# Low and high parts for two more small products, a later place for them, and another order of the low parts, in a four-layer kernel on one core

## Chip, cores and metric

The kernel runs on one core of a Trainium2 chip, in one launch. The metric is the device time of that core in microseconds (us), median over runs. TensorE is written PE in the profile, VectorE DVE, ScalarE ACT, GpSimd POOL and SyncE SP.

## What is computed

The input `x` has 4 sequences of 1024 tokens with 512 features, all float32. Four layers with residual sums follow each other. Cut to what matters here:

```python
x = x + L0(x)     # 512 -> 2048 -> 512, gelu, a part of fc2 chosen per sequence
x = x + L1(x)     # 512 -> 512, weight chosen per sequence
x = x + L2(x)     # below
x = x + L3(x)     # 512 -> 512, weight chosen per sequence

# L2
wg = sigmoid([x, ema(x)] @ Wg.T + bg);  gated = x * wg
h1 = gelu(x @ Wn1.T + bn1)                            # 128 wide
mod = 0.5 + sigmoid(h1 @ Wn2.T + bn2)                 # 4 rates
traces[d] = ema_d(gated * mod[d])                     # 4 scans along the tokens
temporal = sum_d softmax(blend)[d] * traces[d]
gate = sigmoid(temporal @ Wtemp.T + btemp)
soma = gelu(x @ Wsoma.T + bsoma)
out = (soma * gate) @ Wout.T
return (out - mean(out)) / sqrt(var(out) + 1e-5) * gamma + beta
```

## The kernel before

Features lie on the 128 partitions, in 4 chunks, and tokens in the free dimension, in 8 tiles of 512 tokens (tiles 0 to 7, `LAST` is 7). A float32 product is made of three products of a faster kind: each operand is split into a high part (`hi`, rounded by ACT) and a low part (`lo`, the rest, by a subtraction on DVE), and `split_product` adds hi*hi, hi*lo and lo*hi in one bank of PSUM (lines 1623 to 1625). Every engine's program is written out by hand in the order in which it runs, and waits on semaphores for the others.

L0 and L1 of all tiles come first, up to about 690 us. Then L2 and L3 run in rounds. Round r (the loop `for r in range(2, NT)` stands in the programs of ACT and DVE, `range(1, NT)` in that of PE) holds, on PE: `n1(r)` (x @ Wn1), `gate(r, 0)` with the small product `mo(r)` (h1 @ Wn2) in it, the temporal layer `te` of tile r-1, `gate(r, 1)`, `gate(r, 2)`, L3 of tile r-2, `gate(r, 3)`, `ou` of tile r-1, `so(r)` and, between its banks, `ss(r-1)`, a product with ones that sums the squares of `out` over the features. A `gate(i, m)` takes 12 products for one half of the tokens, 12 for the context and 12 for the other half, each 256 wide.

On DVE a round has the four scans of each of 4 chunks (`traces_a` to `traces_d`: `gated_of`, and for each rate `drive_of`, `trace_of`, `add_of`), and between them the low parts, `spikes` (soma * gate, which frees a bank of `te`), `sum_squares`, and `z_of` and `x3_of` for the output of the layer. For the first tile of a sequence `trace_of` starts from zero, for the second from the last column of the first (`trace_last`).

What is not split before: `mo` of tiles 0, 1 and 2 (line 1780, plain float32, as soon as `h1` is there) and `ss` of tile 0 (line 1958). For tiles 3 to 7 `mo` is split: ACT makes `h1_hi` (L1181), DVE `h1_lo` (`h1_low`, L2119). It stands behind the 12 context products of `gate(i, 0)`, not ahead of them. `temporal_low(r, 0)` and `temporal_low(r, 2)` make the low parts of chunks 0, 1 and of chunks 2, 3 of `temporal`; `te_part` waits for the pair that holds its chunk. `te(i, m)` goes through all four chunks for one bank m. The high parts are `temporal_hi(r, m)`. In the profile digits are left out of names: `h` is `h1`, `h_hi` is `h1_hi`, `h_lo` is `h1_lo`, `wn_hl` stands for `wn1_hl` and `wn2_hl`.

The modulation goes to the other engines through DRAM: ACT makes `mod_row` (`mod_of`, `modulation_out`), stores it, and loads it into `mod_t` for all partitions (`modulation_back`, L1200). `drive_of` waits for that load. Two waits of PE at the change: `gate(r, 1)` waits for `spikes(r-1, 0)`, and `l1(LAST, 0)`, L1 of the last tile, which follows `gate(1, 0)`, waits for the four `x1_lo(LAST, c)`.

Of the kernel before, what the change touches and what calls it, by code (L numbers as in the profile page):

```python
# [5 lines left out]
F32 = mybir.dt.float32  # L6
# [37 lines left out]
def build(nc, x, tok16, tok8, small, fc1_w, fc2_w, exp_w, exp_b, l1_w, l1_b, wg, wn1, wsoma, wtemp, wout,  # L44
# [16 lines left out]
    with ctx:  # L61
# [419 lines left out]
        def ss_bank(i):  # L481
            return bank[5 if i == LAST - 1 else 0]
# [27 lines left out]
        def mo_split_no(i):  # L510
            return max(0, i - 2)

        def ss_split_no(i):
            return i
# [440 lines left out]
        def _(eng):  # L955
# [58 lines left out]
            modulation_back(0)  # L1014
            last_columns(0, 0)
# [4 lines left out]
            on.wait_ge(s_made, len(MADE))  # L1020
            eng.memset(wn2_hl[:, :, :].bitcast(F32), 0.0).then_inc(s_wn2, 1)
# [4 lines left out]
        def _(eng):  # L1026
# [151 lines left out]
            def h1_hi_of(i):  # L1178
                on.wait_ge(s_h1, i + 1)
                on.wait_ge(s_pe["SS"], i - 1)  # L1180
                eng.activation(h1_hi[:, :], h1[:, :], ACT.Copy).then_inc(s_h1hi, 1)  # L1181
# [76 lines left out]
            def o_of(i, m):  # L1258
                ps = te_bank(m)
                on.wait_ge(s_pe["OU"], KC * i + m + 1)  # L1260
                if 0 < i < LAST - 1:
                    on.wait_ge(s_pe["L3"], KC * i)
                elif i == LAST - 1:
                    on.wait_ge(s_pe["WG"], KC * NT)
                elif i == 0:
                    for c in range(KC):
                        on.wait_ge(s_hl7[c], 16)
                if i == LAST:
                    if m == 0:
                        on.wait_ge(s_pe["SS"], LAST)  # L1270
                    on.wait_ge(s_add, SH * KC * NT)
                    eng.activation(square_of(i, m), ps[:, :], ACT.Square).then_inc(s_sq, 1)
                    eng.activation(o_of_tile(i)[:, m, :], ps[:, :], ACT.Copy).then_inc(s_o, 1)
                    return
                eng.activation(o_of_tile(i)[:, m, :], ps[:, :], ACT.Copy).then_inc(s_o, 1)
                on.wait_ge(s_o, KC * i + m + 1)
                if m == 0:
                    if i:
                        on.wait_ge(s_pe["SS"], i)
                        on.wait_ge(s_pe["MO"], min(i + 2, NT))  # L1280
                    eng.activation(sumsq[:, :], ps[:, :], ACT.Square).then_inc(s_sq, 1)
                else:
                    if i == LAST - 1:
                        on.wait_ge(s_pe["WG"], KC * NT)
                    eng.activation(square_of(i, m), ps[:, :], ACT.Square).then_inc(s_sq, 1)
# [206 lines left out]
            for c in range(KC):  # L1492
                x1_hi(LAST, c)
            h1_of(1)
            mod_of(1)
# [23 lines left out]
            on.wait_ge(s_wn2, 1)  # L1519
            eng.activation(wn2_hl[:, 0, 0:TAUS], wn2_sb, ACT.Copy).then_inc(s_wn2, 1)  # L1520
            soma_of(1, 0)
            soma_of(1, 1)
# [6 lines left out]
            for r in range(2, NT):  # L1529
                if r == 2:  # L1530
                    h1_of(r)
                    temporal_hi(r - 1, 3)
                else:
                    temporal_hi(r - 1, 3)
                    h1_of(r)
                    h1_hi_of(r)
# [81 lines left out]
        def _(eng):  # L1618
# [151 lines left out]
            def mo(i):  # L1770
                if i > 2:

# [13 lines left out]
            def gate(i, m):  # L1786
# [43 lines left out]
                if m == 0 and i:  # L1830
                    gate_tokens(i, m, 0, 1)
                    if i < 3:
                        mo(i)
# [5 lines left out]
                if m == 0 and i > 2:  # L1839
                    mo(i)  # L1840
# [29 lines left out]
            def te_two(i, m, chunks=range(KC)):  # L1870
                for b in (m, m + 1):
                    if b >= HALF:
                        on.wait_ge(s_soma, KC * i + b + 1)
# [70 lines left out]
            def ss(i):  # L1944
# [6 lines left out]
                if i:  # L1951
                    on.wait_ge(s_ssqhi, ss_split_no(i))
                    eng.matmul(ss_bank(i)[:, :], ones[:, :], sumsq_hi_of(i), start=True, stop=False)  # L1953
                    on.wait_ge(s_ssqlo, ss_split_no(i))
                    eng.matmul(ss_bank(i)[:, :], ones[:, :], sumsq_lo[:, :], start=False, stop=True  # L1955
                               ).then_inc(s_pe["SS"], 1)
                    return
                eng.matmul(ss_bank(i)[:, :], ones[:, :].bitcast(F32), sumsq[:, :], start=True, stop=True
# [112 lines left out]
            for r in range(1, NT):  # L2071
                if r > 1:
                    n1(r)
                    gate(r, 0)
                    for m in range(KC):
                        te(r - 1, m)
# [38 lines left out]
        def _(eng):  # L2115
# [565 lines left out]
            traces_d(0, 3)  # L2681
# [9 lines left out]
            first_traces(1, 0)  # L2691
            x2_of(LAST, 3)
            first_sum(1, 0)
# [19 lines left out]
            traces_c(1, 2)  # L2713
# [3 lines left out]
            traces_c(1, 3)  # L2717
            traces_d(1, 3)
            on.wait_ge(s_wn2, 2)
            low_part(wn2_hl[:, 1, 0:TAUS], wn2_sb, wn2_hl[:, 0, 0:TAUS]).then_inc(s_wn2, 1)  # L2720
            temporal_low(1, 0)
            temporal_low(1, 2)
            for r in range(2, NT):
                if r > 2:
                    h1_low(r)
# [42 lines left out]
                if r == LAST:  # L2768
                    temporal_low(r, 0)
                traces_d(r, 3)  # L2770
                if r < LAST:
                    temporal_low(r, 0)
# [96 lines left out]
```

## Time and profile before

| | |
|---|---|
| median of 3 runs | 1280.25 us (1280.19 to 1282.09) |
| profiled execution | 1279.87 us, span of its trace 1278.1 us |
| PE busy | 1268.8 us, 99% of the span |
| DVE busy | 1067.0 us, 83% |
| ACT busy | 721.6 us, 56% |
| POOL busy | 79.6 us, 6% |
| granted PE clock | 0.999 of full speed |

The page's second part shows that DVE is fuller in the second half, with 9 tenths and more in most slices from 23 on. A product's own row shows it from its start to a modelled end and overlaps the next; how long the engine spends on it is read from start to start.

### The profile page before, as it was taken

The numbers are of one execution on the slowest core, as the hardware profiler recorded it, in microseconds if no ns is written. First come the engines' busy times: TensorE is split into PE (matmuls) and PEld (weight loads), VectorE is DVE, ScalarE is ACT, GpSimd is POOL, SyncE is SP. The second block draws the span as 40 slices with busy tenths as digits, with TensorE's granted clock in tenths as the row PEclk, the third lists the DMA queues.
The fourth block names the chain that finished last, engine by engine and source line by source line (L and its number), as shares of the span: only waits on it lengthen the run. The fifth ranks groups of instructions, "written<-read, shape, count | busy, mean of one in ns | idle before, by whom it ended". The sixth has DMA issues, their size and how long they took to land. (4 is left out here: it accounts for less than half of the span.)

```text
span 1278.1 us, 17514 instructions
## 1 busy us (share of the span) xinstructions
PE 1268.8 (99%) x6109; PEld 1066.8 (83%) x6109; DVE 1067.0 (83%) x1685; ACT 721.6 (56%) x1371; POOL 79.6 (6%) x118
## 2 busy tenths in 40 slices
PE   9999999999999999999999999999999999999998
PEld 7788888888888888888888888888888888888887
DVE  7977777787786987786875898999999999998984
ACT  7577565776475875475765253453636353636355
POOL 0010000000000000000001211002100210021000
PEclk9999999999999999999999999999999999999999
DMA  8357653648744657644749887956467555754401
GB/s 294 103 167 236 191 182 132 222 158 255 225 163 150 239 181 255 201 169 148 239 137 354 306 332 264 391 209 238 174 212 265 196 217 196 260 202 167 140 17 67
DMA packets 115151, 263.68 MB, mean 206 GB/s; under 512 B 10440, under 2 KB 32968, under 8 KB 109944
## 3 DMA queue, kind: packets, MB, share of 16 engines
q1 hardware_dynamic: 95200, 184.32, 42.1%
q10 hardware_dynamic: 15032, 62.45, 13.9%
q0 software_dynamic: 4832, 15.79, 3.3%
q8 instruction: 49, 0.80, 0.3%
q14 instruction: 38, 0.31, 0.1%
HBM read 182.24 MB, written 80.28 MB: 205 GB/s over the span
## 5 line engine op out<-in xcount | busy, mean ns | idle before, releaser
L1623 PE MATMUL bank<-h_hl,w_hl 128*128 128x512 f32 x512 | 199.4, 389 | 0.0
L1624 PE MATMUL bank<-h_hl,w_hl 128*128 128x512 f32 x512 | 199.2, 389 | 0.0
L1625 PE MATMUL bank<-h_hl,w_hl 128*128 128x512 f32 x512 | 199.2, 389 | 0.0
L1623 PE MATMUL bank<-t_hi,sp_hl 128*128 128x512 f32 x448 | 175.2, 391 | 3.2 <-DVE u_sb L2176 1.0
L1624 PE MATMUL bank<-t_lo,sp_hl 128*128 128x512 f32 x448 | 174.4, 389 | 0.0
L1625 PE MATMUL bank<-t_hi,sp_hl 128*128 128x512 f32 x448 | 174.4, 389 | 0.0
L1623 PEld LDWEIGHTS bank<-h_hl,w_hl 128*128 128x128 f32 x512 | 96.1, 188 | 21.0 <-issue 1.2
L1625 PEld LDWEIGHTS bank<-h_hl,w_hl 128*128 128x128 f32 x512 | 96.1, 188 | 20.1
L1624 PEld LDWEIGHTS bank<-h_hl,w_hl 128*128 128x128 f32 x512 | 96.1, 188 | 19.8
L1623 PEld LDWEIGHTS bank<-t_hi,sp_hl 128*128 128x128 f32 x448 | 84.1, 188 | 24.0 <-issue 2.2
L1625 PEld LDWEIGHTS bank<-t_hi,sp_hl 128*128 128x128 f32 x448 | 84.1, 188 | 17.6
L1624 PEld LDWEIGHTS bank<-t_lo,sp_hl 128*128 128x128 f32 x448 | 84.1, 188 | 17.1
L2356 DVE SCALAR_TENSOR_TENSOR drive<-gated,small_sb,mod_t 128x512 f32<-128x512 f32 x128 | 92.5, 744 | 3.3 <-DVE gated L2343 0.7
L2119 DVE TENSOR_TENSOR w_hl<-w_raw,w_hl 128x512 fp32r<-128x512 f32 x128 | 86.7, 685 | 4.3 <-ACT w_hl L1067 3.9
L1134 ACT ACTIVATE h_hl<-hb_in 128x512 fp32r<-128x512 f32 x64 | 40.2, 628 | 82.3 <-DMA hb_in<-hb_dram 55.4
L1067 ACT ACTIVATE w_hl<-w_raw 128x512 fp32r<-128x512 f32 x128 | 78.3, 619 | 6.3 <-PE bank L1625 6.3
L2367 DVE TENSOR_TENSOR_SCAN drive<-alpha,trace_last,drive 128x512 f32<-128x512 f32 x64 | 80.2, 1275 | 0.5
L2367 DVE TENSOR_TENSOR_SCAN drive<-alpha,drive 128x512 f32<-128x512 f32 x64 | 76.4, 1214 | 0.4
L1000 POOL COPY trace_last<-drive 128x1 f32<-128x1 f32 x64 | 48.1, 752 | 412.5 <-DVE drive L2367 411.1
L1051 ACT ACTIVATE sp_hl<-s_raw_sb 128x256 fp32r<-128x256 f32 x128 | 50.9, 411 | 38.4 <-PE bank L1625 36.9
L1624 PE MATMUL bank<-x_slot,wg_hl 128*128 128x256 f32 x256 | 72.4, 283 | 0.0
L1625 PE MATMUL bank<-x_slot,wg_hl 128*128 128x256 f32 x256 | 72.4, 283 | 0.0
(236 smaller groups left out, 3053.9 us busy)
## 6 DMA issues: line engine op xcount, KB each, us to landing
wg_hl<-wg_dram ACTq DMA_DIRECT2D x24, 1536.0 KB, 8.3
fc_raw<-in_fc_w SPq DMA_DIRECT2D x32, 512.0 KB, 4.1
hb_dram<-hb_out SPq DMA_DIRECT2D x64, 256.0 KB, 2.3
hb_in<-hb_dram ACTq DMA_DIRECT2D x64, 256.0 KB, 4.2
x2hl_dram<-x_hl POOLq DMA_DIRECT2D x28, 512.0 KB, 5.4
x_slot<-x2hl_dram SPq DMA_DIRECT2D x26, 512.0 KB, 4.4
wg_hl<-wg_dram SPq DMA_DIRECT2D x8, 1536.0 KB, 8.9
stage<-in_l_w SPq DMA_DIRECT2D x32, 256.0 KB, 3.4
```

What stands on the lines that cost most here:

```text
L1000: eng.tensor_copy(trace_last[:, TAUS * c + d:TAUS * c + d + 1], traced[:, TOK - 1:TOK]).then_inc(s_tracel, 1)
L1051: eng.activation(sp_hl[n % RING][:, 0, :, :], product_source(n), ACT.Copy).then_inc(s_shi, 1)
L1067: eng.activation(w2_hl[v % 3][:, 0, :, :], w2_raw[:, j, :, :], ACT.Copy).then_inc(s_w2hi, 1)
L1134: eng.activation(h_hl[v % 4][:, 0, :], hb_in[v % 4][:, :], ACT.Copy).then_inc(s_hhi, 1)
L1623: eng.matmul(ps, w_hi, x_hi, start=first, stop=False, skip_group_check=resumed)
L1624: eng.matmul(ps, w_hi, x_lo, start=False, stop=False, skip_group_check=resumed)
L1625: return eng.matmul(ps, w_lo, x_hi, start=False, stop=final, skip_group_check=resumed)
L2119: return eng.tensor_tensor(lo, raw, hi.bitcast(F32), ALU.subtract)
L2356: eng.scalar_tensor_tensor(drive[d % 2][:, :], gated[:, :], blend_sb[:, TAUS * c + d:TAUS * c + d + 1], mod_t[:, d, :], ALU.mult, ALU.mult ...
L2367: eng.tensor_tensor_scan(traced, alpha[:, 1 + d:2 + d].to_broadcast([P, TOK]), traced, start, ALU.mult, ALU.add).then_inc(s_trace, 1)
```

## The change

1. `mo` of tiles 1 and 2 is split and stands behind the context products, as that of the later tiles. That needs `h1_hi(1)` and `h1_hi(2)` on ACT, `h1_low(1)` and `h1_low(2)` on DVE, and the split of Wn2 (`wn2_hl`) before `mo(1)`: the memset on POOL, the copy on ACT and the subtraction on DVE move ahead.
2. `ss(0)` is split: `sumsq_hi(0)` on ACT between `soma_of(1, 0)` and `soma_of(1, 1)`, `sumsq_low(0)` on DVE behind `trace_of(1, 2, 2)`.
3. `te` of tile 1 (round 2) goes by two banks at a time, chunk by chunk (`te_two`), as the last tile's does.
4. On DVE `temporal_low(r, 0)` moves ahead of `traces_d(r, 3)`, and `h1_low(r + 1)` from the start of the next round to between `traces_d(r, 3)` and `temporal_low(r, 2)`. On ACT `h1_of(r)` and `h1_hi_of(r)` move ahead of `temporal_hi(r - 1, 3)`. For tile 1 the order is `h1_low(2)`, `temporal_low(1, 0)`, `traces_d(1, 3)`, `temporal_low(1, 2)`.
5. On ACT two of the four `x1_hi(LAST, c)` go behind `h1_of(1)` and `h1_hi_of(1)`; on DVE `x2_of(LAST, 3)` goes between two scans.

```diff
 def mo(i):                                  # PE
-    if i > 2:
+    if i:
         on.wait_ge(s_wn2, 3)
         on.wait_ge(s_h1hi, mo_split_no(i))
...
                 if m == 0 and i:
                     gate_tokens(i, m, 0, 1)
-                    if i < 3:
-                        mo(i)
...
-                if m == 0 and i > 2:
+                if m == 0 and i:
                     mo(i)
...
-                    for m in range(KC):
-                        te(r - 1, m)
+                    if r == HALVES:
+                        te_two(r - 1, 0)
+                        te_two(r - 1, 2)
+                    else:
+                        for m in range(KC):
+                            te(r - 1, m)
...
             for m in range(KC):                                          # DVE
                 x1_of(LAST, m)
-            traces_d(0, 3)
+            on.wait_ge(s_wn2, 2)
+            low_part(wn2_hl[:, 1, 0:TAUS], wn2_sb, wn2_hl[:, 0, 0:TAUS]).then_inc(s_wn2, 1)
+            trace_of(0, 3, 3)
+            h1_low(1)
+            add_of(0, 3, 3)
...
             sum_squares(0)
-            traces_c(1, 2)
+            trace_of(1, 2, 2)
+            sumsq_low(0)
+            drive_of(1, 2, 3)
+            add_of(1, 2, 2)
...
             traces_c(1, 3)
+            h1_low(2)
+            temporal_low(1, 0)
             traces_d(1, 3)
-            on.wait_ge(s_wn2, 2)
-            low_part(wn2_hl[:, 1, 0:TAUS], wn2_sb, wn2_hl[:, 0, 0:TAUS]).then_inc(s_wn2, 1)
-            temporal_low(1, 0)
             temporal_low(1, 2)
             for r in range(2, NT):
-                if r > 2:
-                    h1_low(r)
...
-                if r == LAST:
-                    temporal_low(r, 0)
+                temporal_low(r, 0)
                 traces_d(r, 3)
                 if r < LAST:
-                    temporal_low(r, 0)
+                    h1_low(r + 1)
                     temporal_low(r, 2)
```

DVE at the end of tile 1 (`h_lo` is `h1_low(2)`, the `alpha,trace_last` row is `trace_of(1, 3, 3)`, the `o_sb` row is `z_of(0, m)`), as one piece of the difference:

```order
 L2378 TENSOR_TENSOR temporal<-drive_106,temporal 128x512
-L2367 SCALAR_TENSOR_TENSOR drive_107<-alpha,trace_last,drive_107 128x512
-L2378 TENSOR_TENSOR temporal<-drive_107,temporal 128x512
-L2119 TENSOR_TENSOR wn_hl<-small_sb,wn_hl 128x4
-L2119 TENSOR_TENSOR temporal_lo<-temporal,ts_hi 128x1024 x2
+L2119 TENSOR_TENSOR h_lo<-h_92,h_hi 128x512
+L2119 TENSOR_TENSOR temporal_lo<-temporal,ts_hi 128x1024
+L2367 SCALAR_TENSOR_TENSOR drive_107<-alpha,trace_last,drive_107 128x512
+L2378 TENSOR_TENSOR temporal<-drive_107,temporal 128x512
+L2119 TENSOR_TENSOR temporal_lo<-temporal,ts_hi 128x1024
 L2442 SCALAR_TENSOR_TENSOR o_sb<-o_sb,small_sb,rstd 128x512 x4
```

The last two low parts stood together behind the scan and its add; now one stands ahead of the scan, with `h1_low(2)`, and the other directly behind the add.

PE at `mo(2)` before (the row from `h_92` is `mo(2)`; `x_slot` rows are the token products and `ctx_slot` rows the context products of `gate(2, 0)`):

```order
L1624 MATMUL bank<-x_slot_100,wg_hl_108 128x256
L1625 MATMUL bank<-x_slot_100,wg_hl_108 128x256
L1780 MATMUL bank<-h_92,small_sb 4x512
L1623 MATMUL bank<-ctx_slot_101,wg_hl_108 128x256
L1624 MATMUL bank<-ctx_slot_101,wg_hl_108 128x256
```

And PE at the same place of the changed kernel:

```order
L1625 MATMUL bank<-ctx_slot_104,wg_hl_108 128x256
L1626 MATMUL bank<-ctx_slot_104,wg_hl_108 128x256
L1624 MATMUL bank<-h_hi,wn_hl 64x512
L1625 MATMUL bank<-h_lo,wn_hl 64x512
L1626 MATMUL bank<-h_hi,wn_hl 64x512
L1624 MATMUL bank<-x_slot_97,wg_hl_108 128x256
```

One plain product became three of the split kind, and they stand 12 context products later.

## Rows read from the trace of the kernel before

**Rows 1.** Waits of PE from 660 us on: total us, times, longest us

```profile
PE bank L1623 <- DVE h_lo L2119: 0.9, 1, 0.9
PE bank L1780 <- ACT h L1175: 0.2, 1, 0.2
```

**Rows 2.** Busy us of each engine in one stretch, PE clock, DMA share

```profile
822.40:858.70 36.30, 36.30 (x173) 29.30 (x171) 35.20 (x46) 18.91 (x30) 0.00 (x0) 1.00 0.68 259
```

**Rows 3.** Timeline of PE around the modulation of tiles 2 and 4: start, duration

```profile
843.43 0.28 PE L1624 MATMUL bank<-x_slot,wg_hl 128*128 128x256 f32 x1
843.55 0.28 PE L1625 MATMUL bank<-x_slot,wg_hl 128*128 128x256 f32 x1
...
844.94 0.28 PE L1624 MATMUL bank<-ctx_slot,wg_hl 128*128 128x256 f32 x1
...
976.47 0.39 PE L1623 MATMUL bank<-h_hi,wn_hl 128*64 128x512 f32 x1
...
977.16 0.28 PE L1623 MATMUL bank<-x_slot,wg_hl 128*128 128x256 f32 x1
```

**Rows 4.** Timeline of PE around the sums of squares of tiles 0 and 2

```profile
832.94 0.40 PE L1625 MATMUL bank<-x_slot,wsoma_hl 128*128 128x512 f32 x1
...
834.27 0.40 PE L1624 MATMUL bank<-x_slot,wsoma_hl 128*128 128x512 f32 x1
...
964.94 0.39 PE L1953 MATMUL bank<-ts_hi,ones 128*128 128x512 f32 x1
...
965.41 0.40 PE L1623 MATMUL bank<-x_slot,wsoma_hl 128*128 128x512 f32 x1
```

**Rows 5.** Timeline of PE at gate(2,1), at mo(3) and at gate(3,1)

```profile
858.38 0.39 PE L1625 MATMUL bank<-ts_hi,wtemp_hl 128*128 128x512 f32 x1
858.81 0.36 PE L1623 MATMUL bank<-ctx_slot,wg_hl 128*128 128x256 f32 x1
...
910.48 0.28 PE L1625 MATMUL bank<-ctx_slot,wg_hl 128*128 128x256 f32 x1
911.64 0.41 PE L1623 MATMUL bank<-h_hi,wn_hl 128*64 128x512 f32 x1 [0.87 <-DVE h_lo L2119]
...
924.74 0.28 PE L1623 MATMUL bank<-ctx_slot,wg_hl 128*128 128x256 f32 x1
```

**Rows 6.** Timeline of DVE, end of tile 1 to spikes(2,0)

```profile
845.37 0.69 DVE L2378 TENSOR_TENSOR temporal<-drive,temporal 128x512 f32<-128x512 f32 x1
...
846.05 2.35 DVE L2119 TENSOR_TENSOR temporal_lo<-temporal,ts_hi 128x1024 fp32r<-128x1024 f32 x2
848.32 2.74 DVE L2442 SCALAR_TENSOR_TENSOR o_sb<-o_sb,small_sb,rstd 128x512 f32<-128x512 f32 x4
...
854.18 0.70 DVE L2335 TENSOR_TENSOR bank<-bank,q_sb 128x512 f32<-128x512 f32 x1 [0.48 <-ACT q_sb L1210]
...
857.98 1.28 DVE L2419 SCALAR_TENSOR_TENSOR soma<-bank,soma 128x512 f32<-128x512 f32 x2
...
910.80 0.68 DVE L2119 TENSOR_TENSOR h_lo<-h,h_hi 128x512 fp32r<-128x512 f32 x1
...
921.32 1.28 DVE L2419 SCALAR_TENSOR_TENSOR soma<-bank,soma 128x512 f32<-128x512 f32 x2
```

**Rows 7.** Timeline of ACT at temporal_hi(1,3) and modulation_back(2)

```profile
846.09 0.63 ACT L1231 ACTIVATE ts_hi<-temporal 128x512 fp32r<-128x512 f32 x1 [2.92 <-DVE temporal L2378]
...
852.47 0.81 ACTq L1200 DMA_DIRECT2D mod_t<-mod_dram  x2
```

**Rows 8.** Timeline of DVE ahead of L1 of the last tile

```profile
776.73 1.22 DVE L2367 TENSOR_TENSOR_SCAN drive<-alpha,drive 128x512 f32<-128x512 f32 x1
...
778.59 1.89 DVE L2119 TENSOR_TENSOR x_hl<-x_raw,x_hl 128x512 fp32r<-128x512 f32 x3
```

**Rows 9.** Timeline of PE at the first product of L1 of the last tile

```profile
782.06 0.40 PE L1623 MATMUL bank<-x_hl,l_hl 128*128 128x512 f32 x1
```

**Rows 10.** Transfers that touch mod_t, issue to landing, all of the kernel

```profile
DMA to landing us min/median/max: 3.8/4.8/7.3
```

More of the change, by code:

```diff
@@ L510, in mo_split_no @@
         def mo_split_no(i):
-            return max(0, i - 2)
+            return i
         def ss_split_no(i):
-            return i
+            return i + 1
         def sumsq_hi_of(i):
@@ L1014, in _ @@
             modulation_back(0)
+            on.wait_ge(s_made, len(MADE))
+            eng.memset(wn2_hl[:, :, :].bitcast(F32), 0.0).then_inc(s_wn2, 1)
             last_columns(0, 0)
@@ L1019, in _ @@
                 last_columns(0, c)
-            on.wait_ge(s_made, len(MADE))
-            eng.memset(wn2_hl[:, :, :].bitcast(F32), 0.0).then_inc(s_wn2, 1)
             for i in range(HALVES, NT, HALVES):
@@ L1179, in h1_hi_of @@
                 on.wait_ge(s_h1, i + 1)
-                on.wait_ge(s_pe["SS"], i - 1)
+                if i > 1:
+                    on.wait_ge(s_pe["SS"], i - 1)
                 eng.activation(h1_hi[:, :], h1[:, :], ACT.Copy).then_inc(s_h1hi, 1)
@@ L1279, in o_of @@
                         on.wait_ge(s_pe["SS"], i)
-                        on.wait_ge(s_pe["MO"], min(i + 2, NT))
+                    on.wait_ge(s_pe["MO"], min(i + 2, NT))
                     eng.activation(sumsq[:, :], ps[:, :], ACT.Square).then_inc(s_sq, 1)
@@ L1491, in _ @@
             soma_of(0, 3)
-            for c in range(KC):
-                x1_hi(LAST, c)
+            on.wait_ge(s_wn2, 1)
+            eng.activation(wn2_hl[:, 0, 0:TAUS], wn2_sb, ACT.Copy).then_inc(s_wn2, 1)
+            x1_hi(LAST, 0)
+            x1_hi(LAST, 1)
             h1_of(1)
+            h1_hi_of(1)
+            x1_hi(LAST, 2)
+            x1_hi(LAST, 3)
             mod_of(1)
@@ L1518, in _ @@
             o_of(0, 3)
-            on.wait_ge(s_wn2, 1)
-            eng.activation(wn2_hl[:, 0, 0:TAUS], wn2_sb, ACT.Copy).then_inc(s_wn2, 1)
             soma_of(1, 0)
+            sumsq_hi(0)
             soma_of(1, 1)
@@ L1529, in _ @@
             for r in range(2, NT):
[L1530 to L1536, printed above, removed]
+                h1_of(r)
+                h1_hi_of(r)
+                temporal_hi(r - 1, 3)
                 mod_of(r)
@@ L1870, in te_two @@
             def te_two(i, m, chunks=range(KC)):
+                if m == 0 and i < LAST:
+                    on.wait_ge(s_std, i)
                 for b in (m, m + 1):
@@ L1949, in ss @@
                     on.wait_ge(s_soma, KC * LAST + 2)
[L1951 to L1958, printed above, removed]
+                on.wait_ge(s_ssqhi, ss_split_no(i))
+                eng.matmul(ss_bank(i)[:, :], ones[:, :], sumsq_hi_of(i), start=True, stop=False)
+                on.wait_ge(s_ssqlo, ss_split_no(i))
+                eng.matmul(ss_bank(i)[:, :], ones[:, :], sumsq_lo[:, :], start=False, stop=True
                            ).then_inc(s_pe["SS"], 1)
@@ L2690, in _ @@
             x2_of(LAST, 2)
-            first_traces(1, 0)
+            trace_of(1, 0, 0)
             x2_of(LAST, 3)
+            trace_of(1, 0, 1)
             first_sum(1, 0)
```

## The prediction

> **What bounds the kernel now.** I read first who waited for whom on PE. From 660 us on, where all of the change lies, PE has only two named waits: 0.9 us for `h1_lo` and 0.2 us for `h1` [rows 1]. So the time is PE's work, and small stalls show only as steps between starts. I therefore read PE's timeline from start to start at the places that the change touches. Products 256 wide follow each other by 0.12 us (843.43 to 843.55) [rows 3]; products 512 wide by 0.23 us, as the split sum of squares with two of them shows (964.94 to 965.41, 0.47) [rows 4].
>
> Then I read DVE in the same stretch, since it makes every low part. Between 822.4 and 858.7 us it is busy 35.2 of 36.3 us [rows 2], and its timeline names one idle time, 0.48 us [rows 6]. PE is busy all through. Here both engines are full, and an operation added to DVE is not hidden by idle time of DVE. That decides this case.
>
> **What PE gains.** Modulation of tile 2, plain: from the last token product (843.55) to the second context product (844.94) pass 1.39 us, and two products 256 wide are in it, so it costs 1.39 - 0.24 = 1.15 us. Split, it takes 976.47 to 977.16 = 0.69 us [rows 3]. Two tiles: 2 x 0.46 = 0.92 us. Sum of squares of tile 0, plain: 832.94 to 834.27 = 1.33, with two products 512 wide in it, so 0.87 us; split 0.47 [rows 4]: 0.40 us. Stalls that the new order could take away: 0.2 us ahead of `mo(1)` [rows 1], 858.81 - 858.38 - 0.23 = 0.20 us at `gate(2,1)`, and 911.64 - 910.48 - 0.12 = 1.04 us at `mo(3)` [rows 5]. If nothing else ended last, all of it would be 0.92 + 0.40 + 0.20 + 0.20 + 1.04 = 2.76 us.
>
> **L1 of the last tile.** DVE gets two operations ahead of the four `x1_lo`: the low part of Wn2, 4 columns (I take 0.1 us), and `h1_low(1)`. Equal operations of this form start (1.89 - 0.69) / 2 = 0.60 us apart [rows 8]. The fourth `x1_lo` now ends at 778.59 + 3 x 0.60 + 0.69 = 781.08; then it ends at about 781.78. From the end of `h1_lo` (910.80 + 0.68) to PE's start (911.64) pass 0.16 us [rows 5, 6], so `l1(LAST,0)` can start at 781.9. It starts at 782.06 now [rows 9], so PE gains 0.15 us there, not the 0.66 us of its cheaper `mo(1)` and of the 0.2 us. The memset and the copy of Wn2 lie in idle time of POOL and ACT and cost nothing; without that cover the copy would cost PE at most its own few tenths. What hangs on `mo(1)` (the modulation's way through DRAM) shifts by under 1 us, and DVE then waits for PE again at L1's banks.
>
> **Round 2.** Three things are added to DVE between the last place where it waits for PE (about 822 us) and `spikes(1,0)`, which `gate(2,1)` waits for:
>
> - `sumsq_low(0)`: 0.61 us, by the spacing above (0.60) and a little.
> - `h1_low(2)`: 0.61 us.
> - A round trip to ACT. Now `temporal_low(1,0)` covers it: the add starts at 845.37 and ends at 846.06, ACT makes the high part of chunk 3 from 846.09 for 0.63 us, to 846.72, and DVE is on the first low part by then, from 846.05 [rows 6, 7]. After the change nothing stands between the add and `temporal_low(1,2)`. It starts at about 846.72 + 0.11 = 846.83 on the old clock, and without a wait it would be 845.37 + 0.60 = 845.97: 0.86 us. The Wn2 operation that was there goes away: -0.08. Net 0.78 us.
>
> `temporal_low(1,0)` itself is only moved (1.13 us each: two of them fill 846.05 to 848.32). The sum is 0.61 + 0.61 + 0.78 = 2.00 us later for `z_of(0,0)` and all behind it. The 0.48 us idle at 854.18 doesn't absorb it: there DVE waits for `q_sb`, which stands on ACT behind copies of `x3_of`, so behind DVE's own work. With the lead of 0.15 us from L1, `spikes(1,0)` and `gate(2,1)` come 1.85 us later than now: 858.81 + 1.85 = 860.66. PE's cheaper products of round 2 are spent waiting, first at `mo(2)` and then, by nearly 2 us, at `gate(2,1)`. The two-bank order lets `te` of tile 1 wait for `temporal_low(1,2)` until after 12 products (2.7 us) and not 6; it hides that lateness, but nothing beyond, since `gate(2,1)` sets the time anyway.
>
> **Round 3.** `h1_low(3)` loses one `temporal_low` ahead of it, 1.13 us. It would start at 910.80 - 1.13 = 909.67, end at 910.35, and PE could go on at 910.51, while it arrives at 910.48 + 0.12 = 910.60 [rows 5, 6]. So the 1.04 us at `mo(3)` do go away, with 0.1 us to spare. Bounds: 0.3 to 1.04 us, if ACT's `h1_hi(3)` were late.
>
> DVE doesn't get faster by this; it is 1.0 us and a few tenths closer behind PE from there on. The next wait of PE for it has room: `spikes(2,0)` starts at 921.32 and takes some 0.65 us, and `gate(3,1)` starts at 924.74 [rows 5, 6], 2.8 us later. In the later rounds the new order costs DVE only what the ACT trip is longer than `h1_low` (0.2 us a round), and PE's waits there are none now. I take nothing.
>
> **Sum.** -0.15 + 2.00 - 1.04 = +0.8 us. On the profiled execution's 1279.87 us that is 1280.7 us; the median of the runs shown lies 0.38 us above that execution, so 1281.0 us, 0.06% slower, which is no difference that can be told. A measurement of this kernel tells about 0.2%, 2.6 us, from no change.
>
> The page "VectorE: DVE Perf Modes" of the Trainium skill (section "The DRAIN you can't avoid") says that the next operation doesn't start until the pipe is empty; taken at its word an added low part would cost its whole 0.69 us. The trace doesn't agree: equal operations start 0.60 us apart. By the page the sum would be about 0.2 us higher.
>
> **Rivals.**
>
> - *PE alone counts.* The added DVE work finds room, the waits fall, and PE's 2.76 us come through: 1277.5 us, just at the border of what can be told. For it: the profile calls PE 99% busy. Against it: DVE's 35.2 of 36.3 us [rows 2]. A part of it (round trip hidden, so -0.8) gives about 1280.2, still no difference. Chance that it shows as faster 0.08, of the part 0.17.
> - *The modulation's way through DRAM becomes the end of it.* On ACT `mod_of(2)` now stands behind `temporal_hi(1,3)`, which is 2 us late, so the row is stored 2 us later than now; the load is issued at about 852.47 + 1.85 = 854.3. Transfers into `mod_t` land 3.8 to 7.3 us after their issue, median 4.8 [rows 7, 10], and the drive behind it is due some 4.2 us after the issue. At the median it adds 0.6 us (1281.6), at the maximum 3.1 us (1284.1). It makes the kernel measurably slower from a landing of about 6.0 us on. Chance of that 0.07.
> - *The clock.* PE would stand still for nearly 2 us at `gate(2,1)`, longer than the 0.9 us at `mo(3)`, after which the granted clock stayed at 1.00. Were it to fall to 1.2 GHz, products would take twice as long; from 3.6 us at that level on, 1.8 us are lost and with the +0.8 the kernel is slower by more than 0.2%. Chance 0.02. The Trainium skill ("TensorE: Matmul & The Clock Gate", "Part 1: The HAM clock gate") names idle time as what lowers it; no row here shows the lower level.
> - That the change does something else than it says is excluded by the order shown.
>
> **Numbers.** My case (within 0.2%) 0.66, the partial gain 0.17, the full gain 0.08, the two slower ones 0.09. My own case spans 1280.3 to 1281.8. The range takes in the partial and nearly the full gain below and half of the slower case above: 1277.6 to 1282.9. Faster by over 0.2% 0.08, within 0.83, slower 0.09.
>
> **What would show it.** `gate(2,1)` starts some 1.8 us later against `n1(1)` than now, with a wait for `spikes(1,0)` of nearly 2 us; a wait of under 1 us for `h_lo` at `mo(2)`; a wait of some 0.5 us for `x1_lo` at L1 of the last tile; an idle time of DVE of about 0.8 us ahead of the second `temporal_lo` of tile 1; no wait at `mo(3)`; from round 4 on the same spacing as before. I am wrong if `gate(2,1)` doesn't wait, if `mo(3)` still does, or if a later round shows a wait that is not there now.

## The result and the profile after

The changed kernel takes 1282.33 us (median of 17 runs, 1281.82 to 1285.26), the kernel before 1280.25 us (17 runs beside it). The ratio is 1.0019 with an interval of 1.0013 to 1.0026: 0.19% slower, just inside of what I had called no measurable difference, and above the 1281.0 us forecast. The profiled execution took 1283.01 us, with a span of 1281.3 us.

Busy time has hardly moved (page, first part):

```profile
PE 1269.0 (99%) x6111; PEld 1068.3 (83%) x6111; DVE 1068.5 (83%) x1688; ACT 723.4 (56%) x1374; POOL 79.8 (6%) x118
```

The waits of PE from 660 us on are where the difference shows (total us, times, longest us; the view of [rows 1]):

```profile
PE bank L1624 <- DVE soma L2419: 1.9, 1, 1.9
PE bank L1624 <- DVE h_lo L2119: 0.6, 1, 0.6
PE bank L1624 <- DVE temporal_lo L2119: 0.5, 1, 0.5
PE bank L1624 <- DVE x_hl L2119: 0.2, 1, 0.2
```

The two waits of [rows 1] are gone and four others stand there. Here is the timeline of PE at these places, and at `mo(3)` (914.11 and 914.23; compare [rows 3, 5, 9]):

```profile
782.09 0.50 PE L1624 MATMUL bank<-x_hl,l_hl 128*128 128x512 f32 x1 [0.24 <-DVE x_hl L2119]
...
844.74 0.28 PE L1626 MATMUL bank<-ctx_slot,wg_hl 128*128 128x256 f32 x1
845.64 0.41 PE L1624 MATMUL bank<-h_hi,wn_hl 128*64 128x512 f32 x1 [0.62 <-DVE h_lo L2119]
...
858.66 0.39 PE L1626 MATMUL bank<-ts_hi,wtemp_hl 128*128 128x512 f32 x1
860.94 0.35 PE L1624 MATMUL bank<-ctx_slot,wg_hl 128*128 128x256 f32 x1 [1.89 <-DVE soma L2419]
861.14 0.28 PE L1625 MATMUL bank<-ctx_slot,wg_hl 128*128 128x256 f32 x1
...
862.21 0.42 PE L1624 MATMUL bank<-ctx_slot,wg_hl 128*128 128x256 f32 x1
862.43 0.41 PE L1625 MATMUL bank<-ctx_slot,wg_hl 128*128 128x256 f32 x1
...
865.38 0.28 PE L1624 MATMUL bank<-x_slot,wg_hl 128*128 128x256 f32 x1
865.50 0.28 PE L1625 MATMUL bank<-x_slot,wg_hl 128*128 128x256 f32 x1
...
914.11 0.28 PE L1626 MATMUL bank<-ctx_slot,wg_hl 128*128 128x256 f32 x1
914.23 0.39 PE L1624 MATMUL bank<-h_hi,wn_hl 128*64 128x512 f32 x1
...
1229.02 0.39 PE L1626 MATMUL bank<-x_hi,l3w_hl 128*128 128x512 f32 x1
1229.95 0.50 PE L1624 MATMUL bank<-ts_hi,wtemp_hl 128*128 128x512 f32 x1 [0.55 <-DVE temporal_lo L2119]
```

`gate(2,1)` waits from 858.66 to 860.94. Soon after it products 256 wide stand 0.22 us apart (862.21, 862.43) and not 0.12 us; from 865.38 on it is 0.12 us again. 15 products lose 1.4 us in this way. `mo(3)` follows its context product by 0.12 us: its wait is gone. At `te` of the last tile, 1229.02 to 1229.95, a wait stands that wasn't there before.

The windows of the changed kernel (columns as in [rows 2]; the last but two is the granted clock) say what the wide spacing is:

```profile
862.00:865.20 3.20, 3.20 (x17) 3.20 (x16) 3.20 (x4) 1.40 (x4) 0.88 (x1) 0.50 0.25 100
865.20:868.40 3.20, 3.20 (x28) 3.20 (x28) 3.06 (x5) 0.63 (x1) 0.34 (x2) 0.98 0.19 38
```

The granted clock is 0.50 of full speed, i.e. 1.2 and not 2.4 GHz: 17 products in 3.2 us, 28 in the next 3.2 us. Ahead of it PE had stood still for about 2 us (1.89 us by name).

DVE in the same places (compare [rows 6]; `h_lo` at 844.81 is `h1_low(2)`, at 912.98 `h1_low(3)`, at 1172.05 `h1_low(7)`):

```profile
844.81 0.69 DVE L2119 TENSOR_TENSOR h_lo<-h,h_hi 128x512 fp32r<-128x512 f32 x1
845.41 1.22 DVE L2119 TENSOR_TENSOR temporal_lo<-temporal,ts_hi 128x1024 fp32r<-128x1024 f32 x1
846.54 1.28 DVE L2367 TENSOR_TENSOR_SCAN drive<-alpha,trace_last,drive 128x512 f32<-128x512 f32 x1
847.86 0.69 DVE L2378 TENSOR_TENSOR temporal<-drive,temporal 128x512 f32<-128x512 f32 x1
849.32 1.23 DVE L2119 TENSOR_TENSOR temporal_lo<-temporal,ts_hi 128x1024 fp32r<-128x1024 f32 x1 [0.77 <-ACT ts_hi L1232]
850.46 2.73 DVE L2442 SCALAR_TENSOR_TENSOR o_sb<-o_sb,small_sb,rstd 128x512 f32<-128x512 f32 x4
...
860.11 1.28 DVE L2419 SCALAR_TENSOR_TENSOR soma<-bank,soma 128x512 f32<-128x512 f32 x2
...
912.98 0.69 DVE L2119 TENSOR_TENSOR h_lo<-h,h_hi 128x512 fp32r<-128x512 f32 x1 [1.10 <-ACT h_hi L1182]
...
1172.05 0.69 DVE L2119 TENSOR_TENSOR h_lo<-h,h_hi 128x512 fp32r<-128x512 f32 x1 [1.61 <-ACT h_hi L1182]
```

`z_of(0,0)` starts at 850.46 where it started at 848.32, the second `temporal_low` waits 0.77 us for ACT, and in the later rounds DVE waits up to 1.61 us for `h1_hi`. Behind that wait stands PE itself: ACT can make `h1` of the next tile only when PE has done `n1` of it. ACT ahead of `h1_low(7)`:

```profile
1170.62 0.73 ACT L1175 ACTIVATE h<-bank,small_sb 128x512 f32<-128x512 f32 x1 [1.76 <-PE bank L1768]
```

**The budget.** The stretch up to 660 us, whose code is the same, differs by 0.1 to 1.2 us from one profiled execution to another. So I count from the one product that all kernels share, the plain modulation product of tile 0, to the start of the last product: 689.88 to 1273.95 = 584.07 us before, 690.25 to 1277.11 = 586.86 us after, 2.79 us more. By starts of PE at the same products it splits into: L1 of the last tile -0.23 (from its second product on), up to `gate(2,1)` +1.98 (so 1.75 in all), the lower clock +1.49 with the edges of its stretch, `mo(3)` -1.07, `te` of the last tile +0.63, and under 0.1 us of small steps.

### The profile page after: what moved, and what is told of

Its sections match the earlier page's. It is cut to its first block, busy times and chain, and to the rows that moved or that the text cites. A ratio compares the mean times of both kernels' runs of the same rounds, so it can differ in the third digit from the quotient of the medians.

```text
span 1281.3 us, 17527 instructions
## 1 busy us (share of the span) xinstructions
PE 1269.0 (99%) x6111; PEld 1068.3 (83%) x6111; DVE 1068.5 (83%) x1688; ACT 723.4 (56%) x1374; POOL 79.8 (6%) x118
## 4 chain that ended last, share of the span: by engine, by line
PE 84%; DVE 11%; issue 2%; ACT 2%; DMA 1%; POOL 0%; ACTq 0%; DVEq 0%
PE bank L1624 28%; PE bank L1625 28%; PE bank L1626 28%; DVE drive L2367 3%; DVE drive L2356 1%; DVE temporal L2378 1%; DMA hb_in<-hb_dram 1%; DVE w_hl L2119 1%; DVE t_lo L2119 0%; DVE h_hl L2119 0%; DMA x_raw<-in_x 0%; DVE o_sb L2442 0%; DVE gated L2343 0%; DVE x_raw L2271 0%; DMA mod_t<-mod_dram 0%
## 5 line engine op out<-in xcount | busy, mean ns | idle before, releaser
L2119 DVE TENSOR_TENSOR h_hl<-hb_in,h_hl 128x512 fp32r<-128x512 f32 x64 | 43.8, 685 | 36.4 <-ACT h_hl L1134 36.2
```

The lines of the kernel that those rows point to most:

```text
L2119: return eng.tensor_tensor(lo, raw, hi.bitcast(F32), ALU.subtract)
```

## The experiments

All times are medians. The table has three groups (four rows, three, three); each group ran on one chip beside its own runs of the kernel before, so medians are compared within a group. The ratio is the recorded one; it is not always that of the two medians beside it. "From 690" is the stretch of the budget above, less the 584.07 us of before. "Low clock" says whether products at twice the spacing follow `gate(2,1)` in the profiled execution, and in how many of the timed executions the mean clock of the whole run read below 1.000. One such stretch takes about 0.001 off the mean; the kernel before, with none in its profiled execution, reads so in 17 of 87. The profiled execution of the kernel before shows where such a reading can come from: between 1278 and 1280 us, with its last product started at 1273.95, the granted clock is 0.50, where it costs nothing. So a low reading alone doesn't show a slow stretch at `gate(2,1)`.

| kernel | us | before | ratio, interval | from 690 | low clock |
|---|---|---|---|---|---|
| changed, again | 1283.01 | 1280.61 | 1.0015 (1.0006 to 1.0024) | +3.05 | yes, 6 of 11 |
| work in the gap | 1282.72 | 1280.61 | 1.0019 (1.0010 to 1.0028) | +2.41 | no, 4 of 11 |
| `temporal_low(1,0)` back | 1281.20 | 1280.61 | 1.0005 (0.9996 to 1.0014) | +0.91 | no, 2 of 11 |
| round 6 as before | 1282.97 | 1280.61 | 1.0017 (1.0008 to 1.0026) | +2.07 | yes, 10 of 11 |
| `ss(0)` plain | 1281.80 | 1280.17 | 1.0012 (1.0003 to 1.0021) | +0.72 | no, 3 of 11 |
| low parts back from round 3 on | 1282.72 | 1280.17 | 1.0020 (1.0011 to 1.0029) | +2.48 | no, 2 of 11 |
| the same, `ss(0)` plain | 1281.85 | 1280.17 | 1.0013 (1.0004 to 1.0022) | +1.27 | no, 1 of 11 |
| two orders back | 1280.39 | 1280.33 | 1.0001 (0.9992 to 1.0010) | -0.05 | no, 4 of 11 |
| the same, `ss(0)` plain | 1280.12 | 1280.33 | 1.0000 (0.9991 to 1.0009) | -0.31 | no, 2 of 11 |
| before, `h1_low` between | 1280.54 | 1280.33 | 1.0006 (0.9996 to 1.0015) | -0.04 | no, 3 of 11 |

My theory A: DVE's added work makes `gate(2,1)` late by its own 1.8 us, the wait there lets the clock fall, and the new order of the late rounds costs a little more at `te` of the last tile. Its rivals: the new products or their place lower the clock; a wait taken away in a late round only moves.

**The changed kernel again.**

> The changed kernel unchanged, once more. Theory A (the budget read from its trace: 2.0 us of added DVE work and round trip ahead of gate(2,1), 1.5 us because PE's clock halves for about 3 us right behind that wait, 0.6 us at the temporal layer of the last tile, less 0.2 us at L1 and 1.1 us at mo(3)): 2 to 3 us above the kernel before, and the products behind gate(2,1) again 0.21 us apart for a while. Theory B (the slower products were an accident of one execution): the wait of 2 us is there, the slow products are not, and the time is about 1.3 us above the kernel before.

The slow products are there again, and so is the step of 2.28 us at `gate(2,1)`. The step at `te` of the last tile is 1.14 us here (0.93 us in the first profiled execution).

**Products in the gap.** They read weights that lie in SBUF anyway, and their result isn't used.

```diff
                     te_two(r - 1, 2)
+                    on.wait_ge(s_gated, KC * HALVES)
+                    for _ in range(8):
+                        eng.matmul(bank[7][:, :], wtemp_hl[:, 0, 0, 0:P], wout_hl[:, 0, 0, :], start=True, stop=True)
...
                 gate(r, 1)
```

> The changed kernel with 8 products into an unused bank between the temporal layer of tile 1 and gate(2,1), 8 x 0.23 = 1.84 us of work inside a wait of 2.05 us; their result is not used. Theory A with the idle time of PE as the cause of the lower clock: gate(2,1) starts when it did, products behind it stay 0.12 us apart, and the time is 1.5 us below the changed kernel. Theory B (the clock falls for another reason, or not in most executions): same time as the changed kernel. If filling only delayed, the time would be above it.

No product is slow in this execution, which speaks for PE's standing still as the cause and against the split products. One execution doesn't show it, since the fall stays out now and then without the filling too (below); the waits put into the kernel before, further down, do. The 1.4 us didn't come through whole. In this execution the issue of the two `mod_t` transfers held ACT for 1.45 us (0.81 us in [rows 7]), so `q_sb` and `spikes(1,0)` came later, and then a weight transfer was late at `gate(2,2)`. PE's timeline of this kernel, and the window behind its wait at `gate(2,1)`:

```profile
861.35 0.36 PE L1624 MATMUL bank<-ctx_slot,wg_hl 128*128 128x256 f32 x1 [0.72 <-DVE soma L2423]
...
866.09 0.35 PE L1624 MATMUL bank<-ctx_slot,wg_hl 128*128 128x256 f32 x1 [0.20 <-DMA wg_hl<-wg_dram]
```

```profile
862.00:865.20 3.20, 3.20 (x29) 3.20 (x28) 3.20 (x4) 1.80 (x5) 0.47 (x1) 1.00 0.56 241
```

The median is 0.3 us under that of the changed kernel beside it. Issues of this length occur elsewhere (1.34 us once in the kernel before, at 1109.78), so I can't say whether the products in the gap have to do with it.

**`temporal_low(1,0)` back behind the scan.**

```diff
             h1_low(2)
-            temporal_low(1, 0)
             traces_d(1, 3)
+            temporal_low(1, 0)
             temporal_low(1, 2)
```

> The changed kernel with one DVE operation moved: temporal_low(1,0) behind traces_d(1,3) again, so that it covers the trip to ACT. Theory A: DVE is 0.78 us earlier at spikes(1,0); PE waits about 0.8 us at the start of the temporal layer of tile 1 and 0.8 us less in sum at gate(2,1), so the wait there is between 0.3 and 1.2 us and the clock stays: 0.78 + 1.5 = 2.3 us below the changed kernel, the same as the kernel before. If the clock falls all the same: 0.8 us below. Rival (the low parts of tile 1 limit the temporal layer itself): PE's end of it moves by 0.8 us and the time stays that of the changed kernel.

1.8 us less in the median (1281.20 against 1283.01 us) and 2.1 us less in the trace (+0.91 against +3.05). The wait at `gate(2,1)` is 0.5 us, one of 0.75 us stands ahead of `te(1,0)`, and the clock stays. DVE and then PE of this kernel:

```profile
858.82 1.42 DVE L2356 SCALAR_TENSOR_TENSOR drive<-gated,small_sb,mod_t 128x512 f32<-128x512 f32 x2 [0.30 <-DMA mod_t<-mod_dram]
```

```profile
860.98 0.35 PE L1624 MATMUL bank<-ctx_slot,wg_hl 128*128 128x256 f32 x1 [0.51 <-DVE soma L2419]
```

Counted from the plain product of tile 0, `z_of(0,0)` comes 0.87 us earlier than in the changed kernel and `gate(2,1)` only about 0.6 us, since `drive_of` now waits 0.30 us for the load of `mod_t`. So in these traces the exposed trip to ACT costs about 0.6 us at `gate(2,1)` and the lower clock 1.5 us; and once DVE is that much earlier, the modulation's way through DRAM is the next thing that it waits for.

**The end of round 6 as before.**

```diff
-                    h1_low(r + 1)
-                    temporal_low(r, 2)
+                    if r == LAST - 1: temporal_low(r, 2); h1_low(r + 1)
+                    else:             h1_low(r + 1); temporal_low(r, 2)
```

with `temporal_hi(6, 3)` ahead of `h1_of(7)` on ACT.

> The changed kernel with the order of before at the end of round 6 alone (temporal_low(6,2) ahead of h1_low(7) on DVE, temporal_hi(6,3) ahead of h1_of(7) on ACT). Theory A: the 1.6 us that DVE waits for h1_hi(7) go, and with them the 0.55 us wait of PE at the temporal layer of the last tile: 0.6 us below the changed kernel. Rival (that wait comes from the lateness of round 2, carried on): it stays, and the time too.

The step at `te` of the last tile falls from 0.93 us (1.14 us in the second execution) to 0.22 us:

```profile
1229.70 0.39 PE L1629 MATMUL bank<-x_hi,l3w_hl 128*128 128x512 f32 x1
1229.92 0.46 PE L1627 MATMUL bank<-ts_hi,wtemp_hl 128*128 128x512 f32 x1
```

So the mechanism is right in the trace. The median didn't move (-0.04 us). Here 10 of 11 executions have the low reading, against 6 of 11 of the changed kernel; four more of 11 at 1.4 us are 0.5 us, which is about what is missing; that this is the reason is argued from the counts and not shown.

**The sum of squares of tile 0 plain.** `sumsq_hi(0)` and `sumsq_low(0)` go, and `ss(0)` is one plain product again.

> The changed kernel with the sum of squares of tile 0 plain again (the low part on DVE and the high part on ACT go, PE has the plain product back). Theory A (DVE's added work makes gate(2,1) late, and the wait of PE there, 1.9 us, lowers the clock): DVE reaches spikes(1,0) 0.61 us earlier, PE reaches gate(2,1) 0.40 us later, so the wait is 0.9 us; products behind it stay 0.12 us apart; in all 0.6 + 1.5 = 2.1 us less than the changed kernel, a ratio to the kernel before of about 0.9999. The wait for the low part at te of the last tile stays. Rival B (the lower clock comes from the split products themselves or from the place in the program, not from the length of the wait): products behind gate(2,1) are still 0.21 us apart for 3 us, and no more than 0.6 us is won (1.0010).

I missed the wait: it is 1.88 us and not 0.9. DVE comes 0.61 us earlier, as expected, but with it the wait at `mo(2)` goes (0.78 us by the step of PE's starts), which I had forgotten, so PE arrives earlier too. The plain product makes PE 0.4 us later, the wait at `mo(2)` makes it 0.8 us earlier and small steps behind it 0.2 us; together PE is 0.59 us earlier at the last product of `te`. So both ends of the wait move by the same, and it keeps its length. Behind it the clock stays up in this execution. PE's timeline and the window behind it:

```profile
857.97 0.39 PE L1625 MATMUL bank<-ts_hi,wtemp_hl 128*128 128x512 f32 x1
860.23 0.35 PE L1623 MATMUL bank<-ctx_slot,wg_hl 128*128 128x256 f32 x1 [1.88 <-DVE soma L2422]
```

```profile
861.00:864.20 3.20, 3.20 (x29) 3.20 (x28) 3.20 (x4) 1.70 (x4) 0.59 (x1) 1.00 0.29 119
```

So the fall is not certain after such a wait. Theory A's sum fails with its wait, and the profiled execution doesn't bear out rival B either. In the median this kernel stands 1.6 us above the kernel before beside it, the changed one 2.4 and 2.1 us above its own; 3 of 11 executions have the low reading.

**Waits put into the kernel before.** POOL waits for the last product of `te` or `ou`, makes some copies of one column, and PE waits for the last of them.

```diff
+                for stage, n in (("TE", ...), ("OU", ...)):        # POOL, behind tiles 2, 4, 6
+                    on.wait_ge(s_pe[stage], KC * (i + 1))
+                    for k in range(n): eng.tensor_copy(tick column, eps_sb)
...
+                    on.wait_ge(s_wn2, r + 1)                       # PE, ahead of gate(r, 1), r = 3, 5, 7
...
+                    on.wait_ge(s_wn2, r + 2)                       # PE, ahead of so(r, 0)
```

> The kernel before, with six waits put in ahead of gate(r,1) and so(r,0) of rounds 3, 5 and 7: POOL waits for the last product of te or ou, makes one to six small copies of one column, and PE waits for the last of them. Planned lengths, by the copies' 0.65 us and some 0.4 us for the way there and back: 1.7 and 1.0 us (round 3), 2.3 and 3.0 us (round 5), 3.6 and 4.3 us (round 7). Theory A (it is the length of the wait that lowers the clock, wherever it stands): products are at their old spacing behind 1.0 us, and twice as far apart for some 3 us behind each wait of 2.3 us and more; the kernel is longer than before by the waits and 1.5 us for each of them. Rival B (it is something of round 2 of the changed kernel): no slow products anywhere.

Nothing here is of the change; only the waits are. PE's timeline, the first product behind three of the six waits, and the windows behind the last two:

```profile
1059.28 0.38 PE L1629 MATMUL bank<-ctx_slot,wg_hl 128*128 128x256 f32 x1 [1.72 <-POOL tick L1029]
...
1192.06 0.38 PE L1629 MATMUL bank<-ctx_slot,wg_hl 128*128 128x256 f32 x1 [2.05 <-POOL tick L1029]
...
1225.46 0.50 PE L1629 MATMUL bank<-x_slot,wsoma_hl 128*128 128x512 f32 x1 [2.32 <-POOL tick L1029]
```

```profile
1193.60:1196.80 3.20, 3.20 (x17) 3.20 (x16) 2.65 (x4) 1.26 (x3) 0.00 (x0) 0.50 0.00 0
...
1226.00:1229.20 3.20, 3.20 (x15) 2.63 (x14) 3.20 (x4) 0.67 (x1) 0.00 (x0) 1.00 0.00 0
```

The clock fell behind 2.05 us (1.4 us lost) and not behind 2.32 us. The copies were shorter than I had taken them (0.18 us, the first at a gate 1.2 us), so no wait came near 3 us. As written the theory fails: it had a fall behind every wait of 2.3 us and more, and 2.32 us had none. Rival B fails too, since a kernel with nothing of the change has slow products behind 2.05 us. What is left is that a wait of PE can lower the clock by itself, wherever it stands, and that near 2 us it does so or not. A second kernel of the kind had more waits in that region:

> The kernel before with six waits of PE put in again, more of them near 2 us: five, six and seven copies ahead of gate(3,1), gate(5,1) and gate(7,1), one, six and seven ahead of so(3,0), so(5,0) and so(7,0). By the copies' times in the first such kernel (1.2 us for the first one of a wait, if it is slow, 0.18 us for each further) the waits are 2.0 to 2.4 us at the gates and 0.3, 1.0 to 2.3 and 1.2 to 2.5 us at so. Theory A': near 2 us the clock falls in a part of the cases only, whatever the exact length (it fell behind 2.05 us and not behind 2.32 us in the first such kernel): one to three of the five longer waits are followed by products at twice the spacing for some 3 us. Rival: the length decides, and all waits of over 2.1 us are followed by slow products, or none.

```profile
927.97 0.39 PE L1629 MATMUL bank<-ctx_slot,wg_hl 128*128 128x256 f32 x1 [2.11 <-POOL tick L1029]
...
1061.86 0.39 PE L1629 MATMUL bank<-ctx_slot,wg_hl 128*128 128x256 f32 x1 [1.99 <-POOL tick L1029]
...
1196.44 0.38 PE L1629 MATMUL bank<-ctx_slot,wg_hl 128*128 128x256 f32 x1 [2.11 <-POOL tick L1029]
...
1228.46 0.50 PE L1629 MATMUL bank<-x_slot,wsoma_hl 128*128 128x512 f32 x1 [2.44 <-POOL tick L1029]
```

```profile
929.30:932.50 3.20, 3.20 (x16) 3.20 (x16) 2.85 (x4) 1.27 (x3) 0.00 (x0) 0.50 0.02 5
...
1198.00:1201.20 3.20, 3.20 (x29) 3.20 (x28) 2.57 (x4) 1.27 (x3) 0.00 (x0) 1.00 0.00 0
```

Slow stretches follow the first, the second and the fourth, 1.4 to 1.6 us lost behind each; none follows the third, at the length of the first. So the rival, that the length decides, fails here. These two kernels took 1291.77 and 1296.37 us, one execution each.

**The late orders back in all rounds.** `temporal_low(1,0)` behind the scan, and from round 3 on `h1_low(r+1)` behind `temporal_low(r,2)`, while `temporal_low(r,0)` stays ahead of `traces_d(r,3)`; ACT's order is that of before from round 4 on.

> The changed kernel with temporal_low(1,0) back behind traces_d(1,3), and from round 3 on h1_low(r+1) back behind temporal_low(r,2), on ACT temporal_hi(r-1,3) back ahead of h1_of(r) from round 4 on. Theory A: the 1.8 us of the first edit and the 0.65 us at te of the last tile add up, since one lies in round 2 and the other in round 7: no wait of over 0.6 us anywhere from tile 2 on, no slow products, 2.4 us less than the changed kernel, ratio about 0.9997. Rival C (what is taken from a late round comes back at another wait of the same round, as the single undo of the last round suggests, which moved the median by 0.04 us only): the sum is the 1.8 us alone, ratio 1.0003 or above.

Theory A fails here, and the rival is right only in its direction: it had the 1.8 us of the first order kept, and the trace has +2.48 us against +0.91 us with the first order alone put back. The mix is an order of its own. With `temporal_low(r,0)` ahead of the scan and `h1_low` behind, nothing covers the trip to ACT. DVE and then PE of this kernel, at tile 4:

```profile
976.28 1.22 DVE L2122 TENSOR_TENSOR temporal_lo<-temporal,ts_hi 128x1024 fp32r<-128x1024 f32 x1 [0.77 <-ACT ts_hi L1232]
977.50 0.69 DVE L2122 TENSOR_TENSOR h_lo<-h,h_hi 128x512 fp32r<-128x512 f32 x1
```

```profile
978.33 0.42 PE L1627 MATMUL bank<-h_hi,wn_hl 128*64 128x512 f32 x1 [1.52 <-DVE h_lo L2122]
```

So `mo(4)` now waits 1.5 us where `mo(3)` did before. With `ss(0)` plain it comes out 1.2 us better in the trace and 0.9 us in the median, where I had expected no difference:

> The kernel with both orders put back as in the run before it in this list, and the sum of squares of tile 0 plain as well. Theory A: DVE reaches gate(2,1) 0.61 us earlier, PE 0.40 us later; the wait there was 0.5 us and goes to nothing, and PE itself becomes the end: 0.1 us less than with the split sum of squares, i.e. the two are the same. Rival D (DVE alone sets the time of this stretch): 0.6 us less.

Rival D was the better one: 0.7 us of the 1.2 are there at `gate(2,1)`, DVE's 0.61 us and a little, and the rest at `mo(4)` and `mo(6)`, which wait for DVE too (1.52 and 0.39 us before, 1.08 us and none now). PE's 0.40 us for the plain product lie in time in which it would have waited anyway.

**Two orders back.** `temporal_low(1,0)` behind the scan, and the end of round 6 as before; rounds 2 to 5 as in the change.

> The changed kernel with temporal_low(1,0) back behind traces_d(1,3), and at the end of round 6 alone h1_low(7) behind temporal_low(6,2) (on ACT temporal_hi(6,3) ahead of h1_of(7)); rounds 3 to 6 as in the change. Theory A (the three losses are the wait at gate(2,1), the lower clock behind it in a part of the executions, and the low part at te of the last tile): from 660 us on the kernel whose first order was put back stood 0.91 us behind the kernel before, 0.85 us of it at te of the last tile; without that 0.1 us are left, a ratio of 1.0000 to 1.0003. Rival (what was won in a late round is lost at another wait, as in the kernel that put the order back in all rounds): 1.0006 or more.

> The same kernel as the one before it in this list, with the sum of squares of tile 0 plain as well. Theory A: DVE reaches mo(2), te of tile 1 and spikes(1,0) 0.61 us earlier; PE has the plain product's 0.40 us more and loses the wait of 0.78 us at mo(2); so gate(2,1) starts up to 0.5 us earlier and the kernel stands 0.4 us ahead of the kernel before, 0.9997. Rival (PE's 0.40 us comes through): 1.0003.

Both as theory A had it: -0.05 and -0.31 us in the traces (expected +0.1 and -0.4), ratios 1.0001 and 1.0000. The plain `ss(0)` wins 0.8 us at `gate(2,1)` and gives 0.5 us of it back in round 7, where PE, now earlier, waits 0.2 us each at `mo(7)` and at `te`. The three losses (the trip, the lower clock behind it, the last tile) are named, and in the traces they add up: without them the change is worth nothing, with `ss(0)` plain at best 0.2 us in the median, which can't be told from the kernel before.

**`h1_low` between the low parts, in the kernel before.** It is the one thing of the change that I had credited with the whole of the 1.04 us at `mo(3)`.

```diff
-                if r > 2:
+                if r > 4:
                     h1_low(r)
...
                     temporal_low(r, 0)
+                    if r < 4: h1_low(r + 1)
                     temporal_low(r, 2)
```

> The kernel before, with one thing of the change: h1_low(3) and h1_low(4) stand between temporal_low(r,0) and temporal_low(r,2) of the round ahead, not behind both; nothing is added to DVE and ACT's order stays. Theory A (the wait at mo(3) is one low part in the wrong place): the step at mo(3), 1.16 us, falls to 0.12 to 0.2 us, no later wait grows, and the kernel is 1.0 us shorter, ratio 0.9992. Rival E (DVE is as good as the bound in the later rounds, so that PE's wait only moves): 0.6 us or more of it comes back at mo(5) or at te of the last tile, where PE came just in time before, ratio 0.9997 to 1.0000.

Theory A fails in its form: the step at `mo(3)` is still 912.16 - 911.40 = 0.76 us. The low part had been moved early enough, but it waited for ACT. ACT, and DVE behind it:

```profile
909.37 0.63 ACT L1231 ACTIVATE ts_hi<-temporal 128x512 fp32r<-128x512 f32 x1 [2.45 <-DVE temporal L2378]
909.91 0.72 ACT L1175 ACTIVATE h<-bank,small_sb 128x512 f32<-128x512 f32 x1
910.66 0.63 ACT L1181 ACTIVATE h_hi<-h 128x512 fp32r<-128x512 f32 x1
```

```profile
911.32 0.69 DVE L2119 TENSOR_TENSOR h_lo<-h,h_hi 128x512 fp32r<-128x512 f32 x1 [0.85 <-ACT h_hi L1181]
```

`h1_hi(3)` stands behind `temporal_hi(2,3)`, which waits for DVE's add. So DVE's move alone doesn't remove the wait; the change's other move, `h1_of` and `h1_hi_of` ahead of it on ACT, is needed with it (it wasn't tried alone). Of the 0.4 us by which the step is shorter than the 1.16 us of [rows 5] half comes back at `mo(4)`, whose step grows from 0.12 to 0.31 us since `h1_hi(4)` is late in the same way, and the rest in small steps of under 0.2 us; in all nothing is won. Rival E fails too: the loss is not at the places that it named, nor of its size.

## Why the prediction was right in round 2 and short in its size

The range (1277.6 to 1282.9 us) holds the 1282.33 us measured, but not by the sum: I had my own case end at 1281.8 us, and only the share of the slower rivals took the range beyond it. And one sign of being wrong came, a wait in a later round that was not there before. Round 2 is right in mechanism and size; the later rounds and the clock are not.

- **L1 of the last tile**, foretold -0.15 us with PE starting at 781.9: -0.23 us, start at 782.09 in an execution that ran 0.37 us late by then. The wait named there is 0.24 us, not the 0.5 us foretold. Right in the main.
- **Round 2 on DVE**, foretold 2.00 us: 850.46 - 848.32 = 2.14 us, of which 0.15 us is the offset of the execution at this place, so 1.99 us. The exposed trip showed as 0.77 us of idle time, foretold about 0.8. `gate(2,1)` came 1.75 us late against 1.85. The wait at `mo(2)` is 0.62 us, foretold under 1. Right, and the experiment that put `temporal_low(1,0)` back confirms the trip.
- **Round 3**, foretold -1.04 us: -1.07 us. The number is right; the reason was part of it: DVE waited 1.10 us for `h1_hi(3)` there (912.98), which I had not foretold. I had kept 0.3 us as the bound "if ACT's `h1_hi(3)` were late", and without the change's move on ACT just that happens.
- **The later rounds.** Here the first step failed: "In the later rounds the new order costs DVE only what the ACT trip is longer than `h1_low` (0.2 us a round), and PE's waits there are none now. I take nothing." `h1_low(r+1)` now stands ahead of `temporal_low(r,2)` and waits for `h1_hi` up to 1.61 us, with work behind it that would have covered the wait. The trip that I priced began at the add of `temporal`; the one that counts begins at `n1(r+1)` on PE, for which ACT waits 1.76 us before it can make `h1`. It cost 0.63 us at `te` of the last tile, where PE had come just in time before (1226.50 to 1226.80 = 0.30 us). Putting back the end of round 6 took it away.
- **The clock.** The second step, the larger one in the profiled executions: "Chance 0.02." I took the 0.9 us at `mo(3)` as evidence that a wait twice as long does no harm. In the profiled execution, and again in the second one, the wait was followed by 15 products at the lower level, 1.4 us lost. The rival named the price of "3.6 us at that level, 1.8 us"; it was 3.2 us and 1.4 us. The rule of the Trainium skill that I had put beside it ("TensorE: Matmul & The Clock Gate", "Part 1: The HAM clock gate", that idle time lowers the clock) agrees with these traces.
- The rivals of the full or partial gain of PE did not come; neither did the late modulation: in the changed kernel the drive of round 2 waited for no transfer. It was close, though: with `temporal_low(1,0)` put back it waited 0.30 us.

By the traces the excess is 0.8 us as summed, 0.6 us at the last tile, and 1.4 us in the executions whose clock falls. The medians bear this out in part only. Of the 28 executions of the changed kernel the 12 with the low reading all took 1283.01 us or more, and the 16 others all 1282.77 us or less. The others alone have medians of 1282.17 and 1282.43 us, 1.9 and 1.8 us above the kernel before, where 0.8 + 0.6 = 1.4 us is named. So the executions with the low reading raise the two medians by 0.2 and 0.6 us, and some 0.5 us of each stays unexplained.

Not tried alone: the two-bank order of `te` of tile 1, and the split modulation without the rest.

## What to carry to other kernels

When PE and another engine are both full, an operation is only cheaper on PE if the other engine's part of it isn't ahead of PE's next wait; price the split on the slower side. Before you move an operation forward on one engine, look at what stands ahead of its input on the other, and what used to cover the trip between the two. Follow that input back to its source: here it led over ACT to PE's own products of the next tile. And a stall of PE of about 2 us has to be priced with what the clock may take on top, here 1.4 us in a part of the executions.

## What the runs showed of the hardware

- Of ten waits of PE that the traces name with 1.88 to 2.44 us, in six executions of five kernels and at five places (`gate(2,1)`, `gate(3,1)`, `gate(5,1)`, `gate(7,1)`, `so(7,0)`), seven were followed by some 3.2 us at a granted clock of 0.50, three were not (1.88, 2.11 and 2.32 us); behind waits of 1.76 us and less none was. The length alone doesn't decide: the fall followed 1.89 and 2.05 us.
- The lower clock starts with a delay: the first 8 products behind the wait of the changed kernel still ran at full speed (860.94 to 861.85), in its second execution the first 4 (860.71 to 861.14).
- The issue of the two `mod_t` transfers takes 0.81 us of ACT as a rule, and 1.34 to 1.45 us now and then, in the kernel before as well.
- The first copy of POOL behind a long wait took up to 1.24 us, the next ones 0.18 us.
